# A routed two-block kernel: expert results loaded group by group as their units land, with four result buffers

## The chip, the cores and the metric

The kernel runs on one core of a Trainium2 chip. Its engines work side by side: PE (TensorE, matrix products), ACT (ScalarE), DVE (VectorE), POOL (GpSimd) and SP (SyncE, which here only issues transfers); each executes its own program in order and waits on semaphores. The metric is the device time of one execution in microseconds (us), lower is better. 1% is 4.5 us.

## The reference, cut to what matters

The input is 16 sequences of 256 tokens (4096 tokens) of 128 numbers. Two blocks follow one another, each of the form `x = x + s * silu(experts)`, with `s` from an attention-like part and the experts chosen per token, two of eight. The change touches the second block's expert part and its end:

```python
def _L1_ffn_ref(x, Wg, W1, b1, W2, b2):          # F = 512, E = 8, K = 2
    P = softmax(einsum('bsd,de->bse', x, Wg))
    _, topk_idx = top_k(P, 2)
    P_norm = P restricted to the two chosen, divided by their sum
    h = gelu(einsum('bsd,edf->ebsf', x, W1) + b1)
    y_e = einsum('ebsf,efd->ebsd', h, W2) + b2
    return einsum('ebsd,bse->bsd', y_e, P_norm)
...
g = silu(_L1_ffn_ref(xn, ...)); x = x + s * g
```

With the given inputs the eight experts are chosen 1096, 830, 727, 1419, 1359, 728, 1148 and 885 times. A unit is 256 rows of one expert, so they take 5, 4, 3, 6, 6, 3, 5 and 4 units, 36 in all.

## The kernel before

**Routing.** The tokens are handled in 8 groups of 512. For each group the layer norm of the second block gives rows that POOL scatters, through an indirect DMA, into the DRAM tensor `routed`, where each expert has a region. Each token goes to two experts; the one with the lower number is choice 0, the other choice 1. All of this, with the first block and the attention part of the second, lies in the *first pass*, a list called `ORDER` that every engine walks; the first unit of each expert (units 0 to 7) is worked in its last third.

**The loop over units.** The other units follow expert by expert in loops whose bounds are read from a table that DVE writes (`make_table`): expert 6 has units 6 and 29 to 32, expert 7 has units 7 and 33 to 35. For a unit `u`: SP loads its rows into one of the 4 slots of `ring` (L490), once `ring_free` says that the unit four before is done with its slot. DVE copies them to `xu` (`take`, L1610), two units ahead. PE transposes them (L1019) and makes the hidden layer (L1029, `hid`), ACT applies Gelu (L1239), PE makes the second product into `psC` (L1041, `out`; in the first pass `psB`, L1052). The order on PE is hid(u), transpose for u+1, out(u-1). DVE then runs `results_of`: it adds the bias from `psC` to `yb` (L1622), which frees `psC` by `yb_ready`; waits until the buffer of two units before has landed (`y_landed`); reads the rows' places (`y_to`, L1629) and weights (`y_wt`, L1632), which frees the ring's slot; and multiplies by the weights into `yw` (two operations, L1638). POOL then scatters both halves of 128 rows to the DRAM tensor `results` (L703), by choice and token, and counts in `y_landed` that the unit before has landed (L709).

**The ending.** SP issues two dummy loads of the ring (for takes that nobody uses), waits for them, and then, once the units of experts 0 to 6 have landed, loads choice 0 of all eight groups (`res_lower`, L572; 256 KB each) over first-layer weights that are no longer needed. When the last unit has landed (`all_landed`, L728) it loads choice 1 of all eight groups (`res_higher`). PE adds the two in PSUM through a product with the unit matrix (L1090 for choice 0, L1093 for choice 1, each a 128x512 product in two passes), ACT applies Silu (L1267), DVE multiplies with `s1` (L1665) and adds to `x_all` (L1667), and SP writes the group out (L581).

## Time and profile before

| | us |
|---|---|
| median of 3 runs (446.58, 450.25, 451.49) | 450.25 |
| the profiled execution, device time | 446.94 |
| its span in the trace | 445.2 |
| PE busy | 409.0 (92%) |
| DVE busy | 284.5 (64%) |
| ACT busy | 213.8 (48%) |
| POOL busy | 155.7 (35%) |

The span is the time from the first to the last instruction in the trace; 1.7 us of the device time lie outside it. The page cuts the span into 40 slices of 11.1 us: PE is busy for nine tenths or more in nearly all of them, at a granted clock of 1.0 of full speed, up to the last three. Busy time of PE is modelled, so what waits for what is read from the timeline and from the chain of waits.

### The profile page before, as it was taken

How to read it: one execution, taken by the hardware profiler on the slowest of the kernel's cores; microseconds unless marked ns; L12 is line 12 of the kernel's file. 1: busy time of each engine (PE TensorE's matmuls, PEld its weight loads, DVE VectorE, ACT ScalarE, POOL GpSimd, SP SyncE). 2: the span in 40 equal slices, each digit the busy share in tenths (PEclk: the TensorE clock that was granted, in tenths of full speed). 3: DMA queues.
4: the chain of work that ended last, by engine and by line, in shares of the span. 5: the costliest groups of instructions: out<-in, count | busy, mean ns of one | idle time of the engine just before them, and what ended most of it. 6: DMA issues, size and time to landing. Idle time of an engine off the chain costs nothing. (4 is left out here: it accounts for less than half of the span.)

```text
span 445.2 us, 9851 instructions
## 1 busy us (share of the span) xinstructions
PE 409.0 (92%) x2944; PEld 344.6 (77%) x2944; DVE 284.5 (64%) x1137; ACT 213.8 (48%) x525; POOL 155.7 (35%) x215
## 2 busy tenths in 40 slices
PE   7699989999999999999988999888999999999882
PEld 7579777878869779787767779777899999998630
DVE  4889889888887878878867657412233343433327
ACT  3364555565554545543424353333555555555412
POOL 6340015013233340443433011534454555455510
PEclk9999999999999999999999999999999999999998
DMA  7449411154064330131222223321222222222576
GB/s 181 123 114 166 57 40 42 50 170 135 13 192 122 81 79 25 47 83 53 75 54 61 66 51 80 101 80 54 68 71 67 78 71 71 61 77 68 169 275 193
DMA packets 64210, 40.80 MB, mean 92 GB/s; under 512 B 18340, under 2 KB 57128, under 8 KB 64168
## 3 DMA queue, kind: packets, MB, share of 16 engines
q1 hardware_dynamic: 59472, 31.27, 28.2%
q0 software_dynamic: 4352, 8.99, 6.1%
q8 instruction: 21, 0.34, 0.3%
q14 instruction: 21, 0.17, 0.1%
q10 hardware_dynamic: 344, 0.03, 0.1%
HBM read 21.78 MB, written 18.48 MB: 90 GB/s over the span
## 5 line engine op out<-in xcount | busy, mean ns | idle before, releaser
L694 POOL DMA_INDIRECT routed<-send,slot x64 | 64.5, 1008 | 129.1 <-DMA routed<-send,slot 57.5
L703 POOL DMA_INDIRECT results<-nat,y_to x72 | 69.8, 969 | 89.0 <-DVE nat L1638 65.4
L1029 PE MATMUL psA<-xuT,w_all 128*128 128x256 f32 x288 | 68.9, 381 | 3.5 <-ACT h1T L1239 3.2
L1239 ACT ACTIVATE h1T<-psA,b1T 128x256 f32<-128x256 f32 x144 | 63.1, 473 | 12.0 <-PE psB L1052 7.5
L1029 PEld LDWEIGHTS psA<-xuT,w_all 128*128 128x128 f32 x288 | 50.6, 190 | 11.5 <-issue 2.9
L1041 PE MATMUL psC<-w_all,h1T 128*128 128x128 f32 x464 | 56.7, 275 | 1.0 <-DVE nat L1622 1.0
L1610 DVE TENSOR_SCALAR xu<-ring 128x256 f32 (+1 forms) x38 | 11.2, 295 | 71.2 <-DMA ring<-routed 67.0
L1041 PEld LDWEIGHTS psC<-w_all,h1T 128*128 128x128 f32 x464 | 54.1, 192 | 1.3 <-ACT h1T L1239 1.1
L1230 ACT ACTIVATE xuT<-psB 128x256 f32<-128x256 f32 x37 | 14.2, 383 | 61.6 <-PE psB L1019 45.8
L843 PE MATMUL psB<-xnT,w_l 128*128 128x512 f32 x64 | 34.3, 618 | 0.0
L1170 ACT ACTIVATE hg0T<-psB,b1T 128x512 f32<-128x512 f32 x32 | 22.0, 688 | 22.9 <-PE psB L845 22.8
L855 PE MATMUL psB<-w_l,hg0T 128*128 128x128 f32 x256 | 32.7, 281 | 0.2 <-ACT hg0T L1170 0.2
L855 PEld LDWEIGHTS psB<-w_l,hg0T 128*128 128x128 f32 x256 | 31.2, 192 | 1.1 <-ACT hg0T L1170 0.6
L845 PEld LDWEIGHTS psB<-selT,expert_of 128*128 128x128 bf16 x128 | 9.8, 98 | 18.3 <-issue 18.3
L1638 DVE TENSOR_SCALAR nat<-nat,y_wt 128x128 f32 (+1 forms) x72 | 17.5, 283 | 7.7 <-issue 5.6
L1177 ACT ACTIVATE gg<-psB,tok_w 128x128 f32<-128x128 f32 x32 | 9.1, 368 | 25.3 <-PE psB L856 25.3
L746 PE MATMUL psC<-ident 128*128 128x128 f32 x136 | 19.7, 295 | 1.7 <-POOL ident L598 1.7
L746 PEld LDWEIGHTS psC<-ident 128*128 128x128 f32 x136 | 18.2, 209 | 2.3 <-POOL ident L598 1.7
L683 POOL COPY send<-send 128x512 f32<-128x512 f32 x8 | 5.4, 675 | 40.5 <-ACT send L1105 28.6
L1325 DVE BATCH_NORM_STATS2 stats<-x_all 128x6 f32<-128x128 f32 x64 | 13.9, 279 | 5.8 <-DMA x_all<-in_L_attn_x_dram 5.6
L1105 ACT ACTIVATE send<-x_all,shift,rstd 128x128 f32<-128x128 f32 x32 | 13.2, 483 | 8.6 <-DVE shift L1342 6.5
L1622 DVE TENSOR_TENSOR nat<-psC,b_all 128x256 f32<-128x256 f32 x29 | 12.2, 420 | 4.1 <-PE psC L1041 3.7
(289 smaller groups left out, 851.8 us busy)
## 6 DMA issues: line engine op xcount, KB each, us to landing
ring<-routed SPq DMA_DIRECT2D x38, 130.0 KB
inv<-inv_room SPq DMA_DIRECT2D x8, 512.0 KB
w_all<-results SPq DMA_DIRECT2D x15, 256.0 KB, 4.1
routed<-ring SPq DMA_DIRECT2D x24, 130.0 KB, 6.7
n_room<-nT SPq DMA_DIRECT2D x8, 256.0 KB
w_all<-in_L_ffn_W_dram SPq DMA_DIRECT2D x1, 2048.0 KB
out_dram<-x_all SPq DMA_DIRECT2D x8, 256.0 KB, 2.3
results<-nat,y_to POOLq DMA_INDIRECT x72
```

The costliest lines, as they stand in the source:

```text
L694: pool.indirect_dma_start(routed[:, :], bass.IndirectOffsetOnAxis(ap=slot[par][:, c, t:t + 1], axis=0), send[par][:, c, t, :], None).then_ ...
L703: pool.indirect_dma_start(results[:, :], bass.IndirectOffsetOnAxis(ap=y_to[:, par, a:a + 1], axis=0), yw[:, par, a, :], None).then_inc(S[f ...
L746: mm(to, ident[:, :], ident[:, :], start=True, stop=True)
L843: mm(psB[:, j % 2, :], w, xT0[:, :], start=True, stop=False)
L855: mm(o, hg0T[:, j, col(t)], w2_l0[:, j, :], start=(j == 0), stop=False)
L1029: last = mm(psA[:, j // 2, (j % 2) * UNIT:(j % 2 + 1) * UNIT], w1_all[:, e, j * P:(j + 1) * P], xuT[:, :], start=True, stop=True)
L1041: last = mm(psC[:, a, 0:D], h1T[:, k, a * P:(a + 1) * P], w2_all[:, f * JF + k, :], start=(k == 0), stop=(k == JF - 1))
L1170: f(hg0T[:, j, :], psB[:, j % 2, :], ACT.Gelu, bias=b1T[:, HT + j:HT + j + 1]).then_inc(S["hg0_ready"], 1)
L1230: f(xuT[:, :], psB[:, 0, 0:UNIT], ACT.Copy).then_inc(S["xuT_ready"], 1)
L1239: f(h1T[:, j, :], psA[:, j // 2, (j % 2) * UNIT:(j % 2 + 1) * UNIT], ACT.Gelu, bias=b1T[:, n:n + 1]).then_inc(S["gelu_ready"], 1)
L1325: last = v.bn_stats(stats[:, first + t, :], x_all[:, x_first + t:x_first + t + 1, :])
L1638: last = v.tensor_scalar(yw[:, mine, a, :], yb[:, a:a + 1, :], y_wt[:, a:a + 1], None, ALU.mult)
```

## The change

1. **Result buffers**: `yw` has four buffers, not two. DVE waits for the buffer of four units before. `yb` becomes a tile of its own.
2. **`results_of` in another order**: places and weights are read first (the ring's slot is freed before the unit's second product is done), then bias times weight goes to `yb`, and once the product is there one operation per half gives `psC * weight + yb`. `psC` is now freed by the last of these (`yw_ready`), no longer by the bias operation. `yw_ready` counts halves; POOL waits for each half.
3. **The last unit** makes its first half completely, then its second (`half_ps`), and the halves are weighted and sent apart.
4. **Loads of results by group**: DVE notes after each group how many rows experts 6 and 7 hold (`held`) and works out, behind the table, how many units must have landed for each group (`reach`). SP reads these numbers and waits for each. The dummy ring loads are gone; their count is added to the semaphore. By the counts of this input, choice 0 of groups 0 to 7 needs 29, 30, 31, 31, 31, 32, 33, 33 landed units (the last two by the rule that expert 6 must be finished), choice 1 needs 33, 34, 34, 34, 35, 35, 36, 36.
5. **The ending**: group 0 is summed by DVE in SBUF; groups 1 to 7 by PE, the choice 0 part of group 1 ahead of the last unit's second product. ACT writes Silu over the first-layer weights; DVE finishes groups 2 and 3, and 4 and 5, in one operation each (`ENDS`). After group 0 DVE fills the places of up to three dummy units, so that POOL's loop can go in rounds of four; this waits for the count 35. With 36 units POOL sends none of them.

In the tail of PE's program, with names as in the code (`w_all` is the tile of weights over which results are loaded), this stands in before:

```order
L394 REGISTER_ALU
L1041 MATMUL psC<-w_all,h1T 128x128 [waits gelu_ready]
L1041 MATMUL psC<-w_all,h1T 128x128
L394 REGISTER_ALU
L1041 MATMUL psC<-w_all,h1T 128x128 [waits gelu_ready]
L1041 MATMUL psC<-w_all,h1T 128x128
L1090 MATMUL psD<-w_all,ident 128x512 [waits s1_ready,lower_in0]
L1090 MATMUL psD<-w_all,ident 128x512 [waits lower_in1]
```

and this now:

```order
L1136 MATMUL psD<-w_all,ident 128x512 [waits s1_ready,lower_in1]
L409 ISA
L409 ISA [waits yw_ready]
L1079 MATMUL psC<-w_all,h1T 128x128 [waits gelu_ready]
L409 REGISTER_ALU
L1079 MATMUL psC<-w_all,h1T 128x128 [waits gelu_ready]
L409 REGISTER_ALU
L1079 MATMUL psC<-w_all,h1T 128x128 [waits gelu_ready]
L409 REGISTER_ALU
L1079 MATMUL psC<-w_all,h1T 128x128 [waits gelu_ready]
L1079 MATMUL psC<-w_all,h1T 128x128 x4
L1136 MATMUL psD<-w_all,ident 128x512 [waits lower_in2]
```

The choice 0 product of group 1 has moved ahead of the last unit's second product, which now waits for `yw_ready` in place of `yb_ready`; the others still follow it, group 0 has none.

DVE's operations for a unit in the loop of expert 7 stood like this in before (`ISA` and `REGISTER_ALU` rows set registers):

```order
L1610 TENSOR_SCALAR xu<-ring 128x256
L394 ISA
L1622 TENSOR_TENSOR nat<-psC,b_all 128x256 [waits yw_ready,h1_free]
L1629 ISA [waits y_landed]
L1629 ISA
L1629 TENSOR_SCALAR y_to<-ring 128x2
L1632 ISA
L1632 TENSOR_SCALAR y_wt<-ring 128x2
L394 REGISTER_ALU
L394 REGISTER_ALU [waits ring_free]
L1638 ISA [waits yb_ready]
L1638 TENSOR_SCALAR nat<-nat,y_wt 128x128
```

and stand like this now:

```order
L1689 ISA [waits y_landed,yw_ready]
L1689 ISA
L1689 TENSOR_SCALAR y_to<-ring 128x2
L1692 ISA
L1692 TENSOR_SCALAR y_wt<-ring 128x2
L409 REGISTER_ALU
L1697 TENSOR_SCALAR yb<-b_all,y_wt 128x128 [waits ring_free]
L1697 TENSOR_SCALAR yb<-b_all,y_wt 128x128
L409 ISA [waits yb_ready]
L1705 ISA [waits h1_free]
L1705 SCALAR_TENSOR_TENSOR nat<-psC,y_wt,yb 128x128
```

Places, weights and the bias product now stand ahead of the wait for the second product (`h1_free`), and that wait stands directly ahead of the operations that read `psC` (a second pair of rows like the last two follows).

The diff, cut to its core:

```diff
@@ -559,23 +575,39 @@
                     load_unit(u, nc.s_assert_within((u - bounds[e] + FIRST_UNITS) * UNIT + e * REGION,
                                                     e * REGION, e * REGION + tokens))
-            load_unit(bounds[E], 0)
-            load_unit(bounds[E] + 1, 0)
-            wait_on(sp, "unit_in", (bounds[E] + 2) * 16)
+            wait_on(sp, "unit_in", bounds[E] * 16)
             sp.sem_inc(apart, 1)
-            def load_results(c, to, signal):
-                for g in range(groups):
-                    at = c * tokens + g * GW
-                    sp.dma_start(to[g], results[at:at + GW, :].rearrange("(p t) d -> p t d", t=TILES)
-                                 ).then_inc(signal[g], 16)
+            sp.sem_inc(S["unit_in"], 2 * 16)
+            def load_results(c, g, to, signal):
+                at = c * tokens + g * GW
+                sp.dma_start(to[g], results[at:at + GW, :].rearrange("(p t) d -> p t d", t=TILES)
+                             ).then_inc(signal[g], 16)
+            def units_for(g, c):
+                return sp.value_load(reach[0:1, 2 * g + c:2 * g + c + 1], min_val=FIRST_ALL, max_val=MAX_UNITS)
+            sp.wait_ge(reach_ready, 1)
+            for g in range(groups - 2):
+                wait_on(sp, "y_landed", units_for(g, 0))
+                sp.sem_inc(apart, 1)
+                load_results(0, g, res_lower, lower_in)
+            wait_on(sp, "y_landed", units_for(0, 1))
+            sp.sem_inc(apart, 1)
+            load_results(1, 0, res_higher, res_in)
             wait_on(sp, "y_landed", bounds[E - 1])
-            load_results(0, res_lower, lower_in)
-            sp.wait_ge(all_landed, 1)
-            load_results(1, res_higher, res_in)
+            sp.sem_inc(apart, 1)
+            for g in range(groups - 2, groups):
+                load_results(0, g, res_lower, lower_in)
+            for g in range(1, groups - 1):
+                wait_on(sp, "y_landed", units_for(g, 1))
+                sp.sem_inc(apart, 1)
+                load_results(1, g, res_higher, res_in)
+            wait_on(sp, "y_landed", bounds[E])
+            sp.sem_inc(apart, 1)
+            load_results(1, groups - 1, res_higher, res_in)
             for g in range(groups):
                 sp.wait_ge(S["x2_ready"], g + 1)
                 sp.dma_start(out_rows[:, g * TILES:(g + 1) * TILES, :],
...
-            def send_results(u, par):
-                wait_on(pool, "yw_ready", u + 1)
-                pool.sem_inc(apart, 1)
+            def send_results(u, buf):
                 for a in range(HALVES):
+                    wait_on(pool, "yw_ready", u * HALVES + a + 1)
+                    pool.sem_inc(apart, 1)
                     pool.indirect_dma_start(
-                        results[:, :], bass.IndirectOffsetOnAxis(ap=y_to[:, par, a:a + 1], axis=0),
-                        yw[:, par, a, :], None).then_inc(S[f"y_sent{par}"], 16)
+                        results[:, :], bass.IndirectOffsetOnAxis(ap=y_to[:, buf, a:a + 1], axis=0),
+                        yw[:, buf, a, :], None).then_inc(S[f"y_sent{buf}"], 16)
                 if not (isinstance(u, int) and u == 0):
-                    pool.wait_ge(S[f"y_sent{1 - par}"], (u + par) * (8 * HALVES))
+                    pool.wait_ge(S[f"y_sent{(buf - 1) % YBUFS}"], (u - buf + (YBUFS if buf else 0)) * (16 * HALVES // YBUFS))
                     pool.sem_inc(S["y_landed"], 1)
             def unit_work(what, k=0):
...
-            with pool.Fori(FIRST_ALL, pairs_end, 2) as u:
-                send_results(u, 0)
-                send_results(u + 1, 1)
-            pool.wait_ge(S["y_sent1"], pairs_end * (8 * HALVES))
-            pool.sem_inc(all_landed, 1)
+            rounds_end = pool.value_load(table[0:1, 2 * E + 1:2 * E + 2], min_val=FIRST_ALL,
+                                         max_val=MAX_UNITS + YBUFS - 1)
+            assert FIRST_ALL % YBUFS == 0
+            with pool.Fori(FIRST_ALL, rounds_end, YBUFS) as u:
+                for buf in range(YBUFS):
+                    send_results(u + buf if buf else u, buf)
+            pool.wait_ge(S[f"y_sent{YBUFS - 1}"], rounds_end * (16 * HALVES // YBUFS))
+            pool.sem_inc(S["y_landed"], 1)
...
@@ -1034,7 +1069,20 @@
             def out(u, f, e):
-                wait_on(pe, "yb_ready", u)
+                wait_on(pe, "yw_ready", u * HALVES)
+                if e is None:
+                    for a in range(HALVES):
+                        for k in range(JF):
+                            if a == 0:
+                                wait_on(pe, "gelu_ready", u * JF + k + 1)
+                            last = mm(psC[:, a, 0:D], h1T[:, k, a * P:(a + 1) * P],
+                                      w2_all[:, f * JF + k, :], start=(k == 0), stop=(k == JF - 1))
+                            if a == HALVES - 1:
+                                last.then_inc(S["h1_free"], 1)
+                        if a == 0:
+                            last.then_inc(half_ps, 1)
+                    return
                 for k in range(JF):
                     wait_on(pe, "gelu_ready", u * JF + k + 1)
                     for a in range(HALVES):
...
@@ -1077,18 +1125,21 @@
                     bounds.extend(unit_bounds(pe, len(bounds), upto))
             first_pass(pe, work, unit_work)
-            other_units(pe, bounds, hid, out)
-            for g in range(groups):
+            def lower(g):
                 pe.wait_ge(lower_in[g], 16)
-                if g == 0:
+                if g == 1:
                     wait_on(pe, "s1_ready", groups)
-                elif g == 4:
+                elif g == 5:
                     pe.wait_ge(S["xuT_ready"], bounds[E] + 1)
-                elif g == 6:
-                    wait_on(pe, "yb_ready", bounds[E])
+                elif g == 7:
+                    wait_on(pe, "yw_ready", bounds[E] * HALVES)
                 mm(sum_ps_of(g), ident[:, :], res_lower[g], start=True, stop=False)
-            for g in range(groups):
+            other_units(pe, bounds, hid, out, lambda: lower(1))
+            for g in range(2, groups):
+                lower(g)
+            for g in range(1, groups):
                 pe.wait_ge(res_in[g], 16)
                 mm(sum_ps_of(g), ident[:, :], res_higher[g], start=False, stop=True).then_inc(S["sum_ps"], 1)
...
+            act.wait_ge(sum_sb, 1)
+            f(mix1(0, 1), mix1(0, 1), ACT.Silu).then_inc(S["silu1_ready"], 1)
+            for g in range(1, groups):
+                act.wait_ge(S["sum_ps"], g)
+                f(w1_all[:, g, :], sum_ps_of(g), ACT.Silu).then_inc(S["silu1_ready"], 1)
         @block.vector
...
@@ -1542,6 +1592,8 @@
                     link(v.tensor_tensor(pick[:, :, c], choice[:, :, c], twice(place[:, :, :]), ALU.mult))
                     link(v.tensor_reduce(slot_f[:, :, :], pick[:, :, c], AX.X, ALU.add))
                     v.tensor_copy(slot[par][:, :, :], slot_f[:, :, :]).then_inc(S["slots_ready"], 1)
+                    if g < groups - 1:
+                        link(v.tensor_copy(held[:, g, :], filled[0:1, E - 2:E]))
                     if g == groups - 2:
...
+                def per_group(m):
+                    return m.unsqueeze(1).broadcast_to([1, groups - 1, 2])
+                link(v.tensor_tensor(reach_f[:, :, :], held[:, :, :], per_group(region0[0:1, E - 2:E]), ALU.subtract))
+                link(v.tensor_scalar(held_i[:, :, :], reach_f[:, :, :], float(UNIT - 1), None, ALU.add))
+                link(v.tensor_scalar(held_i[:, :, :], held_i[:, :, :], UNIT.bit_length() - 1, None,
+                                     ALU.logical_shift_right))
+                link(v.tensor_scalar(reach_f[:, :, :], held_i[:, :, :], float(FIRST_UNITS), -float(FIRST_UNITS),
+                                     ALU.max, ALU.add))
+                v.tensor_tensor(reach[:, :].rearrange("a (p e) -> a p e", e=2), reach_f[:, :, :],
+                                per_group(bound_f[:, E - 2:E]), ALU.add).then_inc(reach_ready, 1)
             def take(u):
...
@@ -1615,17 +1679,13 @@
                 dve.wait_ge(S["xuT_ps"], u + 2)
                 take(u + 2)
-            def results_of(u, f, ps):
-                wait_on(dve, "h1_free", (u + 1) * JF)
-                wait_on(dve, "yw_ready", u)
-                v.tensor_tensor(yb[:, :, :], ps,
-                                b2_all[:, f:f + 1, :].broadcast_to([P, HALVES, D]),
-                                ALU.add).then_inc(S["yb_ready"], 1)
-                wait_on(dve, "y_landed", u - 1)
+            def results_of(u, f, ps, by_halves=False):
+                wait_on(dve, "yw_ready", u * HALVES)
+                wait_on(dve, "y_landed", u - YBUFS + 1)
                 at = ring[:, bass.ds(u % RING, 1), :, :]
-                mine = bass.ds(u % 2, 1)
+                mine = bass.ds(u % YBUFS, 1)
                 v.tensor_scalar(y_to[:, mine, :].rearrange("p r a -> p (r a)").unsqueeze(2),
                                 at[:, :, :, COL_ID:COL_ID + 1].bitcast(I32)
                                 .rearrange("p r a d -> p (r a) d"), 0.0, None, ALU.add)
@@ -1633,11 +1693,17 @@
                                 .rearrange("p r a d -> p (r a) d"), 1.0, None,
                                 ALU.mult).then_inc(S["ring_free"], 1)
                 wait_on(dve, "ring_free", u + 1)
+                for a in range(HALVES):
+                    last = v.tensor_scalar(yb[:, a, :], b2_all[:, f, :], y_wt[:, a:a + 1], None, ALU.mult)
+                last.then_inc(S["yb_ready"], 1)
                 wait_on(dve, "yb_ready", u + 1)
                 for a in range(HALVES):
-                    last = v.tensor_scalar(yw[:, mine, a, :], yb[:, a:a + 1, :], y_wt[:, a:a + 1],
-                                           None, ALU.mult)
-                last.then_inc(S["yw_ready"], 1)
+                    if a == 0 and by_halves:
+                        dve.wait_ge(half_ps, 1)
+                    else:
+                        wait_on(dve, "h1_free", (u + 1) * JF)
+                    v.scalar_tensor_tensor(yw[:, mine, a, :], ps[:, a:a + 1, :], y_wt[:, a:a + 1], yb[:, a:a + 1, :],
+                                           ALU.mult, ALU.add).then_inc(S["yw_ready"], 1)
             def unit_work(what, k=0):
                 if what == "first":
...
+            def spare_places():
+                wait_on(dve, "yw_ready", bounds[E] * HALVES)
+                for n in range(YBUFS - 1):
+                    wait_on(dve, "y_landed", bounds[E] + n - YBUFS + 1)
+                    mine = bass.ds((bounds[E] + n) % YBUFS, 1)
+                    v.tensor_scalar(y_to[:, mine, :].rearrange("p r a -> p (r a)").unsqueeze(2),
+                                    spare[:, mine, :].rearrange("p r a -> p (r a)").unsqueeze(2), 0.0, None,
+                                    ALU.add).then_inc(S["yw_ready"], HALVES)
+            dve.wait_ge(lower_in[0], 16)
+            dve.wait_ge(res_in[0], 16)
+            v.tensor_tensor(mix1(0, 1), mix1(0, 1), res_higher[0], ALU.add).then_inc(sum_sb, 1)
+            def finish(first, end):
+                ts = slice(first * TILES, end * TILES)
+                m = mix1(first, end)
+                dve.wait_ge(S["silu1_ready"], end)
+                v.tensor_tensor(m, s1[:, ts, :], m, ALU.mult).then_inc(S["mix_ready"], end - first)
+                dve.wait_ge(S["mix_ready"], end)
+                v.tensor_tensor(x_all[:, ts, :], x_all[:, ts, :], m, ALU.add).then_inc(S["x2_ready"], end - first)
             dve.wait_ge(S["s1_ready"], groups)
-            for g in range(groups):
-                finish(g)
+            for first, end in ENDS:
+                finish(first, end)
+                if first == 0:
+                    spare_places()
 # ---- launch: one core; inputs and outputs as the reference has them ----
```

## Rows read from the trace of the kernel before

**Rows 1.** windows at the end: us, busy us (x instructions), clock, DMA share
```profile
400.00:420.00 20.00, 19.04 (x136) 17.18 (x135) 7.27 (x32) 12.23 (x27) 10.23 (x11) 1.00 0.31 93
420.00:430.00 10.00, 7.37 (x17) 2.58 (x16) 1.14 (x5) 0.00 (x0) 3.32 (x4) 1.00 0.71 240
```

**Rows 2.** chain that ended last, in time order: start us, us, what
```profile
424.79 2.24 DMA results<-nat,y_to
...
427.09 2.77 DMA w_all<-results
...
429.91 1.14 PE psD L1093 x2
...
431.07 0.61 ACT hg0T L1267
...
431.77 0.70 DVE hg0T L1665
...
441.79 0.69 DVE x_all L1667
```

**Rows 3.** timeline of SP and PE at the end: start us, us, what
```profile
417.06 3.45 SPq L572 DMA_DIRECT2D w_all<-results  x7
...
417.84 2.05 PE L1041 MATMUL psC<-w_all,h1T 128*128 128x128 f32 x16 [0.96 <-DVE nat L1622]
...
426.20 1.02 PE L1090 MATMUL psC<-w_all,ident 128*128 128x512 f32 x2
...
427.06 1.02 PE L1090 MATMUL psC<-nT,ident 128*128 128x512 f32 x2
```

**Rows 4.** timeline, DVE and POOL around the last two units
```profile
417.31 0.97 POOL L703 DMA_INDIRECT results<-nat,y_to  x1 [0.30 <-issue]
...
418.19 0.48 DVE L1638 TENSOR_SCALAR nat<-nat,y_wt 128x128 f32 x2 [0.24 <-DVE y_wt L1632]
...
419.46 0.97 POOL L703 DMA_INDIRECT results<-nat,y_to  x1 [1.19 <-issue]
...
419.92 0.42 DVE L1622 TENSOR_TENSOR nat<-psC,b_all 128x256 f32<-128x256 f32 x1 [1.25 <-PE psC L1041]
...
420.74 0.96 POOL L703 DMA_INDIRECT results<-nat,y_to  x1 [0.30 <-issue]
421.70 0.17 DVE L1629 TENSOR_SCALAR y_to<-ring  x1 [1.35 <-issue]
```

**Rows 5.** one line of the ending: duration ns min/median/max
```profile
L1665 DVE TENSOR_TENSOR hg0T<-s,hg0T x8: 682/684/691, 431.8 to 441.1; 128x512 f32<-128x512 f32 x8
```

**Rows 6.** timeline, the loop over units: PE, DVE, SP
```profile
321.25 1.95 PE L1041 MATMUL psC<-w_all,h1T 128*128 128x128 f32 x16
...
322.81 0.29 DVE L1610 TENSOR_SCALAR xu<-ring 128x256 f32 x1 [1.91 <-DMA ring<-routed]
...
324.99 1.95 PE L1041 MATMUL psC<-w_all,h1T 128*128 128x128 f32 x16
...
407.43 0.38 SPq L490 DMA_DIRECT2D ring<-routed  x1
...
410.34 0.29 DVE L1610 TENSOR_SCALAR xu<-ring 128x256 f32 x1 [2.39 <-DMA ring<-routed]
...
414.93 1.95 PE L1041 MATMUL psC<-w_all,h1T 128*128 128x128 f32 x16
```

**Rows 7.** timeline, from the first pass into the loop
```profile
306.97 0.30 DVE L1610 TENSOR_SCALAR xu<-ring 128x256 f32<-128x256 f32 x1 [4.87 <-DMA ring<-routed]
...
308.47 1.95 PE L1052 MATMUL psB<-w_all,h1T 128*128 128x128 f32 x16
```

**Rows 8.** page, groups of instructions and DMA issues
```profile
L1638 DVE TENSOR_SCALAR nat<-nat,y_wt 128x128 f32 (+1 forms) x72 | 17.5, 283 | 7.7 <-issue 5.6
...
w_all<-results SPq DMA_DIRECT2D x15, 256.0 KB, 4.1
```

**Rows 9.** timeline of SP, the eight fills
```profile
283.81 8.66 SPq L544 DMA_DIRECT2D routed<-fill  x8
```

68 lines of the change are left out of this document (32 added, 36 removed).

## The prediction

> **What bounds the kernel now.** I read the windows first. Up to 420 us PE is busy nearly without a gap at a granted clock of 1.00, which is the level of 2.4 GHz; from 420 to 430 us it still works for 7.4 us, DVE for 1.1 and ACT for none [rows 1]. So there are two parts: a long one set by PE, and an ending of some 25 us set by something else. The chain of waits says by what [rows 2]: the last scatter of results (issued at 424.79, landed 2.24 us later), the load of choice 1 of the first group (2.77), PE's sum (1.14), Silu (0.61), and then DVE alone: from 431.77 to 442.48 (441.79 + 0.69) it alternates between the two operations of each group. That is 10.71 us for 8 groups, 1.33 a group plus 0.07 for the last dependency. The write of the last group takes the rest of the span, 445.2 - 442.48 = 2.72 us. All eight loads of choice 1 wait for the last unit, although most groups' rows have landed long before; that is where time can be had. The sum below is made on the span (445.2 us); the profiled execution took 446.94.
>
> **The long part.** Four edits act before the last unit.
>
> *The order inside a unit.* In the loop PE starts a second product every 3.75 us (321.25 to 414.93 in 25 periods [rows 6]). DVE's take starts 1.56 us after the start of the product at 321.25; the one at 410.34 is among the late ones, its load issued at 407.43 had taken 2.91 us [rows 6]. Freeing the slot earlier makes this chain shorter: the 0.42 us bias operation no longer stands in it. Only few tenths are there to win, because an undisturbed period is 324.99 - 321.25 = 3.74, and 25 of them are 93.5 us against 93.7 measured. I take -0.2 (bounds -0.4 and 0).
>
> *`psC` comes free later.* Between take and free there now stand places and weights, two bias products and two operations on PSUM. Nearest rows: 128x256 from PSUM 0.42 [rows 4], 128x512 from two tiles 0.68 [rows 5], so 0.27 for 256 columns and about 0.285 for 128; two of them 0.55. A small operation is 0.17 [rows 4], a weighting 0.283 [rows 8]. Take 0.29, two small ones 0.3, two waits on its own results about 0.5, two bias products 0.5, the last pair 0.55: about 2.15 us. Where the take is not late, all but the last pair lies under PE's product (1.95 us), and the pair lies under the hidden product, the other 1.8 us of the period; cost zero. Where the take comes x us after the product's start, PE waits once x + 2.15 exceeds 3.74. That is so at one place that the trace shows: the take at 306.97 had waited 4.87 us for its ring slot's rows, and PE began the next product at 308.47 [rows 7]. Now the bank is free at 306.97 + 2.15 = 309.1: +0.6 us. After it the take falls in step, since from take to take by way of a load it is now about 0.5 to the weights, 0.25 to SP (both estimated from the small operations) and 2.91, under 3.74.
>
> *DVE's additions in the first pass*: seven notes of `held`, five operations for `reach`, and per unit about 0.2 us more (0.57 + 0.57 for the two pairs instead of 0.42 + 0.57, and waits). With 0.25 us each that is 1.75 + 1.25 + 1.4 = 4.4 us on DVE. PE keeps busy beside it, so most is hidden; bounds 0 and 4.4, I take +0.2, nearer to nothing since the `reach` operations stand behind the signal that others wait for.
>
> *Ahead of the last product* the choice 0 sum of group 1 (two passes, 1.02 us; groups on PE stand 0.86 apart) goes where PE waited 0.96 us for `psC`, from 416.9 to 417.84 [rows 3]. The last product starts at 417.9, not 417.84: +0.1.
>
> Sum of the long part: -0.2 + 0.6 + 0.2 + 0.1 = +0.7 us. The last product ends at 420.6 instead of 419.9.
>
> **The ending.** *Scatter.* Unit 34's halves are ready at about 418.1 (416.9 + 0.6 for the shift, 0.55 for the pair), POOL starts them 0.8 later as now (418.19 + 0.48 to 419.46 [rows 4]): 418.9 and, a send taking 1.27 with its gap (419.46 to 420.74), 420.1. The last unit's first half is ready 1 us before the end, at 419.9; POOL is free at 421.3, sends at 421.3 and 422.5. It lands 2.24 later [rows 2], or later when loads share the DMA engines: DVE got the buffer of unit 33, whose second half was sent at 417.31, only at 421.70 [rows 4], 4.39 us later, while eight loads were under way from 417.06 [rows 3]. (That reading is an upper bound: POOL may have counted late.) So the last unit has landed at 424.8 to 426.9; before it was 427.03. The wait of DVE on the buffer (1.35 us [rows 4]) is gone with four buffers.
>
> *Loads.* The SP queue is done with the ring when the last real load has landed, at 410.3 at the latest [rows 6], so choice 0 goes out from then to about 417, and choice 1 of group 0 at about 417. Each dynamic step (a read of `reach`, a wait, an issue) I price by the eight fills, 8.66/8 = 1.08 us [rows 9]; bare issues are 3.45/7 = 0.49 [rows 3]. Groups 1, 2, 3 need 34 units, counted at 420.0 to 420.9: issued by 420.9, 422.0, 423.1. Groups 4 and 5 need 35: 424.2, 425.3. Groups 6 and 7: 426.4 to 427.0, and 0.5 later. Landing is 2.77 for the first [rows 2], 4.1 in the median [rows 8]: groups 1 to 7 are there at 425.0, 426.1, 427.2, 428.3, 429.4, 431.0, 431.6 at the latest.
>
> *PE* has six choice 0 sums to do after 420.6: 6 x 0.86 = 5.2, to 425.8. Then choice 1 of group 1: result at 425.8 + 1.14 = 426.9, the others 0.86 apart, kept back by at most 1 us by the loads.
>
> *DVE* does group 0 (sum 0.69, Silu 0.6, two products) from 421.0 to 423.6 and the spare places (three of 0.17 with register work) to 424.3; the count 35 for which they wait is there by 424.3. It is then idle until Silu of group 1, 426.9 + 0.65 = 427.5. From there: group 1 1.33 (428.8); groups 2 and 3, whose Silu is ready at 429.2: an operation of 1024 columns is 0.68 + 2 x 0.27 = 1.22, two with their dependency 2.4 (431.6); groups 4 and 5 2.4 (434.0); group 6 1.33, group 7 1.40 (436.7). The write 2.72: **439.4**.
>
> So the span falls by 445.2 - 439.4 = 5.8 us: 4.3 because DVE's row starts at 427.5 and not 431.8, 1.5 because it has seven groups and two of its steps are doubled. The profiled execution would take 446.94 - 5.8 = 441.1. The median of the runs shown is 450.25, 3.3 above that execution, with one run (446.58) at its level; scaled by 439.4/445.2 it is 444.4. I say 443.5, between the two and nearer to the scaled median.
>
> **One rule against it.** Scatters and loads delay each other: 2.24 us alone, up to 4.39 beside eight loads [rows 2, 4]. The Trainium skill ("DMA: Bandwidth & Descriptors", section "Issuing engines are not separate DMA queues") says that transfers of all queues run on the same 16 DMA engines and interleave; the trace agrees with 4.39 beside 2.24. The old ending kept the last scatter free of loads, the new one puts it among those of groups 1 to 5. By 2.24 the last group is loaded at 430.1, by 4.39 at 431.6; DVE comes to it at 435.3, which needs the load by 433.5, so both give 439.4.
>
> **Rivals.** (a) *The hidden work of DVE isn't hidden*: in the first pass all 4.4 us lie on the path, or PE waits for `psC` more often. Against it: PE's few gaps there. It gives 439.4 + 4.2 on the span: 445 to 449 by the runs, within 1%. (b) *The last landing decides.* From a landing of group 7 after 433.5, two microseconds past my latest, each further us costs one. The rule above is its mechanism; a scatter of 6.5 us would eat 1 to 2 us: 445. (c) *Slower*: `psC` late in every unit. If a take stays more than 1.59 us behind the product's start, PE waits for the excess each time; at 2.0 behind that is 0.42 x 28 = 12 us, 450.25 + 6 = 456. It needs ring loads that land over 2.98 us after issue in the mean, where the late one took 2.91 [rows 6]; and each such wait gives the loads time to catch up. (d) *More than forecast*: the ring's chain is what makes two of three runs 450 and more; shortened, it takes away 3 us besides: 440. For it the late take at 410.34 [rows 6], against it that no row shows such a loss. (e) *The counts don't come early*, so that the loads go out late as before: all choice 1 loads would again follow the last unit's landing. Against it: two groups of eight need the last unit, the rest up to two units less. It would leave some 2.5 us of the faster scatter and the 1.5 of DVE: 446.
>
> **How the numbers follow.** My forecast 50% (own range 441 to 446.5), (a) 15%, (b) and (e) together 10%, (c) 8%, (d) 17%. The range 438 to 449 leaves out (c) and the far ends of (a) and (d). About 1% (4.5 us) is what a measurement can tell from no change. Faster by over 1%: (d) and most of my forecast, 0.60. Within: the rest of it, (a), (b), (e): 0.32. Slower: 0.08.
>
> **What would show it.** In the profile after: DVE's last row of operations starts near 427.5 + 0 to 1 and lasts 9.2 us without a wait for a DMA (else (b)); PE's first choice 1 sum stands right behind the last choice 0 sum; the start of PE's last product lies near 418.5 (at 422: (a); at 430: (c)); loads of choice 1 go out in three bunches. I am wrong if PE shows waits for DVE's `psC` in the loop, or if its idle time before the choice 1 sums exceeds 1 us each.

## The result: slower by 1.3%, with the ending faster as forecast and the loop slower

The changed kernel takes 453.75 us in the median of 14 runs (451.81 to 457.15), the kernel before 447.88 (445.42 to 451.49, 14 runs). The ratio is 1.0129, 95% interval 1.0098 to 1.016. The forecast was 443.5 (438 to 449) with a chance of 0.08 for slower by over 1%: it was wrong, in sign too. The profiled execution of the changed kernel has a span of 451.6 us, against 445.2.

Where the 6.4 us of span come from, place by place (starts of the same product in both traces):

| place | before | after | cost |
|---|---|---|---|
| first unit's product of the loop starts | 312.7 | 314.95 | +2.3 |
| from there to the loop's 28th product | 102.1 | 112.4 | +10.2 |
| from the 28th to the end of the span | 30.4 | 24.3 | -6.1 |

So the change gained 6.1 us where it was meant to gain, and I had forecast 5.8 for the whole. The loop lost 10.2 us, where I had forecast -0.2. First the ending, in the timeline of the changed kernel; columns as in the same view of before (start us, us, engine and line, what, [idle before <- releaser]); DVE's last line of operations answers [rows 2], the loads [rows 3]:

```profile
430.45 2.05 PE L1079 MATMUL psC<-w_all,h1T 128*128 128x128 f32 x16 [0.22 <-ACT h1T L1290]
...
432.66 7.08 SPq L585 DMA_DIRECT2D w_all<-results  x7
...
434.75 1.13 POOL L737 DMA_INDIRECT results<-nat,y_to  x1 [0.30 <-issue]
...
437.48 1.88 PE L1144 MATMUL psD<-w_all,ident 128*128 128x512 f32 x4
...
439.17 0.69 DVE L1744 TENSOR_TENSOR w_all<-s,w_all 128x512 f32<-128x512 f32 x1 [2.97 <-ACT w_all L1318]
...
440.88 1.13 PE L1144 MATMUL psA<-w_all,ident 128*128 128x512 f32 x2 [0.66 <-DMA w_all<-results]
...
440.96 1.23 DVE L1744 TENSOR_TENSOR w_all<-s,w_all 128x1024 f32<-128x1024 f32 x1 [0.37 <-ACT w_all L1318]
...
448.12 0.69 DVE L1746 TENSOR_TENSOR x_all<-x_all,w_all 128x512 f32<-128x512 f32 x1
```

From the start of the last product to the end of the span it is 451.6 - 430.45 = 21.15 us; before it was 445.2 - 417.84 = 27.36 [rows 3]. PE's first choice 1 sum (437.48) stands behind the last choice 0 sum (436.62, two passes) with no wait, and the only wait of the row on a load is 0.66. DVE's row lasts 448.81 - 439.17 = 9.64 (forecast 9.2), the write 2.79 (forecast 2.72).

Now the loop. One unit of it, in the changed kernel and in the kernel before (the product on `psC` is the second product of the unit before, the one on `psA` the hidden product of the next):

```profile
381.74 1.87 PEld L1089 LDWEIGHTS psC<-w_all,h1T 128*128 128x128 f32 x16
...
382.35 0.96 POOL L737 DMA_INDIRECT results<-nat,y_to  x1 [0.30 <-issue]
...
383.65 2.32 PE L1064 MATMUL psA<-xuT,w_all 128*128 128x256 f32 x8
383.95 0.84 ACT L1290 ACTIVATE h1T<-psA,b1T 128x256 f32<-128x256 f32 x2 [0.35 <-PE psC L1089]
...
384.84 0.73 PEld L1064 LDWEIGHTS psA<-xuT,w_all 128*128 128x128 f32 x4 [0.46 <-ACT h1T L1290]
```

```profile
321.25 1.95 PE L1041 MATMUL psC<-w_all,h1T 128*128 128x128 f32 x16
...
321.90 1.81 ACT L1239 ACTIVATE h1T<-psA,b1T 128x256 f32<-128x256 f32 x4
322.97 0.98 POOL L703 DMA_INDIRECT results<-nat,y_to  x1 [0.30 <-issue]
```

In the kernel before, ACT's four Gelus follow one another with no gap (1.81 for four): each overwrites a quarter of `h1T`, and PE's releases of the quarters (`h1_free`, one at the end of each quarter of the product) come in time. In the changed kernel ACT waits for the third release: 0.35 us in the row, and PE then waits 0.46 for ACT's result. I count time in a unit from the first weight load of the product (here 381.74; 0.10 before the row of the matmuls). The releases are due at +0.74, +1.18, +1.63 and +2.07, and where nothing is late ACT starts a Gelu some 0.02 us behind each. The matmul of the third ends at +1.63, but its signal arrives at +2.14, and ACT's third Gelu starts at +2.21. Half a microsecond is lost in most units: the median period is 4.15 in place of 3.73. The rows that group this, ACT's Gelus between 310 and 415 us (form, count | busy, mean ns | idle before <- releaser), of before and of after:

```profile
L1239 ACT ACTIVATE h1T<-psA,b1T 128x256 f32<-128x256 f32 x112 | 50.3, 473 | 3.6 <-PE psC L1041 1.3 <-PE psB L1052 0.8
```

```profile
L1290 ACT ACTIVATE h1T<-psA,b1T 128x256 f32<-128x256 f32 x100 | 44.0, 472 | 14.9 <-PE psC L1089 11.4 <-issue 1.4
```

ACT's waits for `psC` have grown from 1.3 to 11.4 us, the 10.2 of the loop. I call such a release late. Nothing in my working had a price for it, and PE's rows show no wait for DVE there, which is what I had feared in rival (c).

The 2.3 us ahead of the loop are not the change's, or hardly. Of this execution 1.6 us went into one stretch in which the clock granted to PE was lower (behind it the same operations of DVE stand 1.6 us later than in the two further profiles named below, ahead of it they do not):

```profile
20.00:25.00 5.00, 4.86 (x23) 4.00 (x24) 4.50 (x20) 3.98 (x8) 4.73 (x20) 0.67 0.00 0
```

(windows: us, busy us of PE, PEld, DVE, ACT, POOL, clock, DMA share, GB/s; in the kernel before the clock reads 1.00 there.) In two more profiles of the unaltered changed kernel it reads 1.00 there, and the first product of the loop starts at 312.5 and 312.3, where the kernel before has 312.7.

### The profile page after: what moved, and what is told of

Its sections match the earlier page's. It is cut to its first block, busy times and chain, and to the rows that moved or that the text cites. A ratio compares the mean times of both kernels' runs of the same rounds, so it can differ in the third digit from the quotient of the medians.

```text
span 451.6 us, 10024 instructions
## 1 busy us (share of the span) xinstructions
PE 415.5 (92%) x2940; PEld 345.2 (76%) x2940; DVE 302.2 (67%) x1185; ACT 212.9 (47%) x525; POOL 154.3 (34%) x216
## 4 chain that ended last, share of the span: by engine, by line
PE 61%; DVE 16%; issue 8%; ACT 6%; SPq 4%; DMA 3%; ACTq 1%; DVEq 0%
PE psC L1089 12%; PE psA L1064 10%; PE psB L890 7%; PE psB L878 6%; ACT h1T L1290 2%; DVE stats L1375 2%; DMA ring<-routed 2%; PE psD L1007 2%; PE psB L1054 1%; PE psB L880 1%; PE psA L846 1%; DVE nt_a L1389 1%; PE psC L781 1%; PE psA L860 1%; DVE nt_a L1390 1%
## 5 line engine op out<-in xcount | busy, mean ns | idle before, releaser
L728 POOL DMA_INDIRECT routed<-send,slot x64 | 63.5, 993 | 131.4 <-DMA routed<-send,slot 56.3
L1064 PE MATMUL psA<-xuT,w_all 128*128 128x256 f32 x288 | 75.8, 393 | 6.8 <-ACT h1T L1290 4.7
L1674 DVE TENSOR_SCALAR xu<-ring 128x256 f32 (+1 forms) x38 | 12.5, 329 | 64.0 <-PE psB L1054 47.1
L1089 PE MATMUL psC<-w_all,h1T 128*128 128x128 f32 x448 | 54.6, 275 | 0.0
L1089 PEld LDWEIGHTS psC<-w_all,h1T 128*128 128x128 f32 x448 | 52.2, 192 | 0.0
L1705 DVE SCALAR_TENSOR_TENSOR nat<-psC,y_wt,yb 128x128 f32 x58 | 17.9, 347 | 9.8 <-PE psC L1089 8.8
L1697 DVE TENSOR_SCALAR yb<-b_all,y_wt 128x128 f32<-128x128 f32 x72 | 17.5, 291 | 1.3
```

The costliest lines, as they stand in the source:

```text
L728: pool.indirect_dma_start(routed[:, :], bass.IndirectOffsetOnAxis(ap=slot[par][:, c, t:t + 1], axis=0), send[par][:, c, t, :], None).then_ ...
L1064: last = mm(psA[:, j // 2, (j % 2) * UNIT:(j % 2 + 1) * UNIT], w1_all[:, e, j * P:(j + 1) * P], xuT[:, :], start=True, stop=True)
L1089: last = mm(psC[:, a, 0:D], h1T[:, k, a * P:(a + 1) * P], w2_all[:, f * JF + k, :], start=(k == 0), stop=(k == JF - 1))
L1697: last = v.tensor_scalar(yb[:, a, :], b2_all[:, f, :], y_wt[:, a:a + 1], None, ALU.mult)
L1705: v.scalar_tensor_tensor(yw[:, mine, a, :], ps[:, a:a + 1, :], y_wt[:, a:a + 1], yb[:, a:a + 1, :], ALU.mult, ALU.add).then_inc(S["yw_read ...
```

## The experiments

Eighteen runs were made in five groups, each group on one chip beside the kernel before; five of them repeat a kernel (the changed kernel twice, e1, e2 and e5 once each). The kernel before took 448.2, 448.7, 449.5, 449.6 and 447.3 us on them, which is no difference worth a word. The variants were another matter. Results in one table; "second send" is the place in a unit where POOL starts its second scatter of results, counted as above (its median, or the range that holds 8 units in 10).

| label | chip | ratio to before [95%] | median period | second send |
|---|---|---|---|---|
| e1_old_order | 10 | 0.986 [0.981, 0.991] | 3.73 | +1.5 to +2.3 |
| e2_bias_behind | 10 | 0.989 [0.984, 0.994] | 3.73 | +1.40 |
| e3_slot_late | 10 | 1.021 [1.016, 1.027] | 4.37 | +1.68 |
| e5_order_alone | 10 | 1.0005 [0.997, 1.004] | 3.73 | +1.15 |
| e0_after | 13 | 1.011 [1.008, 1.013] | 4.15 | +0.61 |
| e6_sends_whole | 13 | 1.021 [1.017, 1.025] | 4.36 | +0.9 to +1.2 |
| e8_sends_later | 13 | 1.041 [1.039, 1.044] | 4.64 | +1.47 |
| e9_slot_after_bias | 13 | 1.012 [1.007, 1.017] | 4.17 | +0.6 to +1.6 |
| e1_again | 6 | 1.007 [1.003, 1.011] | 4.03 | +1.57 |
| e2_again | 6 | 1.043 [1.037, 1.048] | 4.64 | +1.44 |
| e5_again | 6 | 1.039 [1.034, 1.044] | 4.43 | +0.88 |
| e7_old_by_halves | 6 | 1.024 [1.019, 1.028] | 4.20 | +0.61 |
| e10_sends_past | 5 | 1.007 [1.003, 1.010] | 4.43 | +2.03 to +2.2 |
| e11_old_sends_past | 5 | 0.997 [0.993, 0.9998] | 3.73 | +2.1 to +3.2 |
| e12_sends_spaced | 5 | 1.046 [1.039, 1.052] | 4.31 | spaced |
| e13_after_third | 5 | 1.013 [1.005, 1.021] | 4.20 | +0.61 |
| e14_sends_pinned | 7 | 0.988 [0.984, 0.991] | 3.73 | +2.94 |
| e15_old_pinned | 7 | 0.987 [0.983, 0.990] | 3.73 | +2.95 |

### First group (chip 10): which part of the change costs the period?

**e1_old_order** puts the order of DVE's steps in a unit back; four buffers, sends by halves, the loads by group and the new ending stay. The diff is shortened.

```diff
-                v.tensor_scalar(yb[:, a, :], b2_all[:, f, :], y_wt[:, a:a + 1], None, ALU.mult)   # bias first
+                v.tensor_tensor(yb, ps, b2_all[f], ALU.add).then_inc(S["yb_ready"], 1)            # frees psC
 ...
-                v.scalar_tensor_tensor(yw[a], ps[a], y_wt[a], yb[a], ALU.mult, ALU.add)
+                v.tensor_scalar(yw[a], yb[a], y_wt[a], None, ALU.mult)
```

> The changed kernel with one part undone: the weighting of a unit is again in the order of before (bias added from psC as soon as the product is there, which frees psC; then places, weights, two weightings). Four buffers, sending by halves, loads by group and the new ending stay. The traces show the loop's period at 3.74 us before and 4.13 after, some 10.6 us over 27 units, while the ending from the start of the last product is 6.2 us shorter (27.4 to 21.2). If the order inside a unit is the cause, the period goes back to 3.74 to 3.78 and the time falls below before by 5 to 7 us: ratio 0.984 to 0.990. If instead the four buffers, POOL's two waits per unit or the loop in rounds of four slow the loop, the period stays at 4.1 and the ratio at 1.01 or above.

Measured: 441.2 us, period 3.73, span 438.5. It looked like a proof that DVE's order makes the release late. And it tests the ending of the forecast with the loop undisturbed: 438.5 against the 439.4 of my sum.

```profile
417.62 1.95 PE L1079 MATMUL psC<-w_all,h1T 128*128 128x128 f32 x16
...
426.25 0.69 DVE L1751 TENSOR_TENSOR w_all<-s,w_all 128x512 f32<-128x512 f32 x1 [1.71 <-ACT w_all L1318]
...
435.02 0.69 DVE L1753 TENSOR_TENSOR x_all<-x_all,w_all 128x512 f32<-128x512 f32 x1
```

DVE's row starts 8.6 us behind the start of the last product (forecast 427.5 - 418.5 = 9.0) and lasts 9.46 (forecast 9.2).

**e2_bias_behind** keeps the new order, but DVE waits for PE's product before it makes the two bias products.

```diff
+                wait_on(dve, "h1_free", (u + 1) * JF)
                 for a in range(HALVES):
                     last = v.tensor_scalar(yb[:, a, :], b2_all[:, f, :], y_wt[:, a:a + 1], None, ALU.mult)
```

> The changed kernel, but DVE waits for the unit's second product before it multiplies the bias by the weights; places and weights are still read early, so the ring slot is freed and SP's load is issued inside PE's product as in the changed kernel. In its trace PE's signal for the third quarter of the product (h1_free) comes 0.5 to 0.58 us late in each unit, while both the two bias products of DVE and SP's issue of the ring load (0.38 us) run. Theory 1 (DVE's bias products delay the signal): the period goes back to 3.74 to 3.80, the time to 5 to 7 us under before, ratio 0.984 to 0.990. Theory 2 (SP's issue delays it): the period stays at 4.1, ratio 1.01 or a little above, since psC comes free 0.5 us later besides.

Measured: 442.2 us, period 3.73. Here SP's issue stands where it stood in the changed kernel, so it could not be the cause; the bias products could.

**e3_slot_late** frees the ring slot only behind the last operation of a unit.

```diff
-                                ALU.mult).then_inc(S["ring_free"], 1)
+                                ALU.mult).then_inc(S["wt_read"], 1)
 ...
+                dve.sem_inc(S["ring_free"], 1)
```

> The changed kernel, but the ring slot is declared free only after the unit's two last operations, so that SP issues the next load outside PE's second product; the bias products stay inside it. Theory 1 (bias products): the signal stays late by 0.5 us and the period at 4.1 us, ratio about 1.01. Theory 2 (SP's issue): the signal comes in time and the period goes back to 3.74 to 3.80, ratio 0.985 to 0.99.

Measured: 457.5 us, period 4.37, and for a reason that neither theory named: no release is late, the ring is. PE waits for `psC` in most units (22 waits, 9.6 us in all, between 310 and 415 us). One of them:

```profile
361.49 2.05 PE L1089 MATMUL psC<-w_all,h1T 128*128 128x128 f32 x16 [0.24 <-DVE nat L1705]
...
363.60 0.29 DVE L1674 TENSOR_SCALAR xu<-ring 128x256 f32 x1 [2.25 <-DMA ring<-routed]
...
365.15 0.61 DVE L1705 SCALAR_TENSOR_TENSOR nat<-psC,y_wt,yb 128x128 f32 x2 [0.25 <-DVE yb L1697]
...
365.89 0.37 PE L1089 MATMUL psC<-w_all,h1T 128*128 128x128 f32 x1 [0.41 <-DVE nat L1705]
```

This is my rival (c) as it was written, brought about on purpose: the take stands 2.11 us behind the product's start, `psC` is free 2.16 us behind the take (365.76; I had worked out 2.15), and PE waits for the excess. In the changed kernel the slot is freed early and the take comes 0.6 behind the start, so it does not happen there.

**e5_order_alone** is the kernel before with the new order of DVE's steps and nothing else.

> The kernel before with one part of the change alone: the new order of places, weights, bias products and the two operations on psC; two buffers, whole units sent, the old loads and the old ending. If the order is the cause (theories 1 and 2 alike) the period is 4.1 us and the time 9 to 12 us over before, ratio 1.02 to 1.027, with the ending as before. If it needs the four buffers or the sends by halves too, the period stays at 3.74 and the ratio near 1.00.

Measured: ratio 1.0005, period 3.73 in all units but two, with the bias products inside PE's product. So the order alone cost nothing on this chip, order and four buffers together (the changed kernel, measured elsewhere) cost 0.42 a unit, and each alone was free. That did not fit any theory I had.

### Second group (chip 13): the sends

What else differs between those kernels is the place of POOL's sends in the unit. It hangs on when a result is ready, on how many buffers there are and on whether the halves are waited for one by one. The group moves the sends, and runs the changed kernel again.

> The changed kernel once more, unaltered, on the chip that also runs the others of this group. The four variants run so far had no late release from PE, the profiles of the kernel before and of the changed one both had some, and those two came from other executions, perhaps another chip. Theory A (the change itself makes PE's third release of each second product late): period 4.15 in the loop, 1.3% above the kernel before (about 454). Theory B (the late releases belong to the chip or the execution, not to the kernel): no late release here, period 3.73, and with the ending's gain about 442.

> The changed kernel, but POOL waits for both halves of a unit before it sends either, as before the change. Its sends start about 0.3 us later in each unit: the second one ends near +1.9 us after the product's start instead of +1.58, where PE's third release is due at +1.63. Theory A1 (the release is late when POOL's send ends just before it): the release is on time or the lateness moves to the fourth release, period 3.73 to 3.9, 442 to 447. Theory A2 (four buffers or DVE's order as such): period stays 4.15, 454.

> The changed kernel, with one read of a word of the table on POOL (about 0.7 us, its value is not used) ahead of each loop unit's first send. Nothing is left out. The second send then runs from about +1.35 to +2.3 us after the product's start, past PE's third release at +1.63, as in the variants without late releases. Theory A1: no late release, period 3.73, about 442 (the ending may lose 1 us: the last unit's sends also start later). Theory A2: period stays 4.15, 454. Theory B: as the unaltered kernel does on this chip.

> The changed kernel, but the ring slot is freed behind the two bias products instead of ahead of them, so SP's issue comes at about +2.05 us after the product's start instead of +1.79, behind PE's third release; POOL's sends and the bias products keep their places. Theory A3 (SP's issue in the 0.2 us behind the release makes it late): release on time, period 3.73 to 3.8, 442 to 445. Theory A4 (the bias products there make it late, SP has no part): period stays 4.15, 454.

The edits: `e0_after` none. The other three:

```diff
 # e6_sends_whole, POOL
+                wait_on(pool, "yw_ready", (u + 1) * HALVES)
                 for a in range(HALVES):
-                    wait_on(pool, "yw_ready", u * HALVES + a + 1)
 # e8_sends_later, POOL, ahead of a unit's first send
+                        pool.value_load(table[0:1, 2 * E + 1:2 * E + 2], ...)
 # e9_slot_after_bias, DVE, behind the two bias products
+                dve.sem_inc(S["ring_free"], 1)
```

Measured: the changed kernel again 4.15, so it was not one odd execution; that the chip has a part in it, the other half of B, is not settled by this group. Both kernels with later sends are slower still, 4.36 and 4.64, so A1 as I had put it falls, and with the slot freed later it stays at 4.17, so A3 falls. But the trace of e8 said more than the time: now it is the fourth release that is late, by 0.95 us, and the third is not.

### Third group (chip 6): the same kernels on another chip

All four of the first group had no late release, all four of the second had some. So three of the first group ran again.

> The first variant (changed kernel with the old order of DVE's steps in a unit) once more. All four variants of the first group ran on one chip and none had a late release from PE in its trace, all four kernels of the second group ran on another chip and all had some. Theory K (it is the kernel's order that decides): again no late release that reaches PE, period 3.73, ratio to the kernel before 0.986. Theory C (it is the chip that decides): on a chip other than the first one, releases of PE are up to 1 us late here too, period 3.9 to 4.2, and the ratio rises to about 1.00 to 1.01.

> The second variant (changed kernel, bias products only behind the wait for PE's product) once more. Theory K: period 3.73, ratio 0.989. Theory C: on a chip other than the first one, late releases and a ratio of 1.00 or more.

> The kernel before with the new order of DVE's steps alone, once more. Theory K: ratio 1.00, period 3.73, no late release. Theory C: on a chip other than the first one, late releases that now reach PE, because DVE's step comes later in the unit: period about 4.1, ratio up to 1.02.

> As the run before it (kernel before, new order of DVE's steps), and the unit's results signalled and sent by halves: POOL's first send starts about 0.3 us earlier in each unit, with two buffers. If sends by halves are what makes the order expensive, this one has late releases and a period of about 4.1 while the one before it does not; if not, both stand at the same period.

Theory C holds, by a wide margin: e2 goes from 0.989 to 1.043, e5 from 1.0005 to 1.039, e1 from 0.986 to 1.007, with the same program. One unit of e2 on chip 10, then on chip 6:

```profile
362.08 1.87 PEld L1089 LDWEIGHTS psC<-w_all,h1T 128*128 128x128 f32 x16
...
362.83 1.81 ACT L1290 ACTIVATE h1T<-psA,b1T 128x256 f32<-128x256 f32 x4
...
363.47 0.97 POOL L737 DMA_INDIRECT results<-nat,y_to  x1 [0.30 <-issue]
```

```profile
361.22 1.86 PEld L1089 LDWEIGHTS psC<-w_all,h1T 128*128 128x128 f32 x16
...
361.97 1.37 ACT L1290 ACTIVATE h1T<-psA,b1T 128x256 f32<-128x256 f32 x3
...
362.65 0.97 POOL L737 DMA_INDIRECT results<-nat,y_to  x1 [0.30 <-issue]
...
364.26 0.47 ACT L1290 ACTIVATE h1T<-psA,b1T 128x256 f32<-128x256 f32 x1 [0.92 <-PE psC L1089]
364.78 0.73 PEld L1064 LDWEIGHTS psA<-xuT,w_all 128*128 128x128 f32 x4 [1.04 <-ACT h1T L1290]
```

POOL's second send is at +1.4 in both. On chip 10 four Gelus run in a row; on chip 6 the fourth waits 0.92 us, and PE after it 1.04. And two kernels of one group differ by their sends only: e5_again has its second send at +0.88 and a period of 4.43, e7 (the same, by halves) at +0.61 and 4.20.

What the chips differ in can be read off the signals that the traces record. I took the events of the loop of all 20 traces and counted them from the start of the second of two sends that follow each other by 1.27 us (pairs 1.25 to 1.30 us apart, whose first send starts between 318 and 410 us); "landing" is a signal of one of a transfer's 16 DMA engines.

| | chips 13, 6, 5, and the first profiles of before and after (14 traces) | chips 10, 7 (6 traces) |
|---|---|---|
| landings of the first send, +0.5 to +1.05 | 3 to 6 recorded (medians) | 16 (9 in e14, where some come later) |
| landings of the second send, near +2.1 (POOL at rest) | 16 | 16 (9 in e2 and 4 in e5, where they come later) |
| signals of any engine or DMA recorded, +0.92 to +1.38 | none in 288 of 291 pairs | some in all 125 |
| PE's releases of all products due +0.6 to +1.3 | 291 of 317 recorded late, near +1.5 to +1.6; 18 without a record | all 144 on time |

On one kind of chip the landing of the first send falls into the running second send, a few of its signals are recorded, and then no signal of anything is recorded for some 0.6 us, until about +1.5 us behind the start of the second send. I call this the silence. A release of the second product that is due in it takes effect at its end: of 69 for which ACT was already waiting (due +0.92 to +1.38), 68 let ACT start late, by 0.34 us in the median.

But it is a silence of the record, and not of all signals. In the unit of the changed kernel shown above DVE's read of the weights ends at 382.93 + 0.35 = 383.28, which is +0.93 behind the second send (382.35). Its signal has no record, yet SP, which waits for it, goes on 0.03 us later and issues the ring's load, while PE's third release is still 0.3 us away:

```profile
383.52 0.38 SPq L506 DMA_DIRECT2D ring<-routed  x1
```

So it is wherever one can look, in the same 14 traces and the same window: 105 signals of DVE for which SP was waiting let it start 25 to 29 ns later, as on the other chips (28 ns); 36 of 41 Gelus for whose end PE was waiting let it start 50 to 52 ns later, as there; and 7 of 9 of PE's own signals of a transpose let ACT start 36 to 38 ns later. None of them has a record. Even outside the window records are missing: in the kernel before, the third release has none in 17 of the 26 units behind the first, and ACT starts its third Gelu on time, at +1.64 to +1.66, in all 26. A missing record thus does not show a late signal; what shows it is the start of the engine that waited. By that, the releases of the second product are late in the silence, and DVE's signals are not. Why these and not the others, the traces do not show.

The rule gives the periods of most kernels: in the changed kernel the second send starts at +0.61, the silence ends at +0.61 + 1.53 = +2.14, the third release was due at +1.63: 0.51 late, of which the period shows 0.42. In e2_again it is +1.44 + 1.58 = +3.02, the fourth was due at +2.07: 0.95 late, the period +0.91. It does not give that of e1_again (4.03): there the second send starts at +1.57 and the fourth release is due 0.50 behind it, ahead of the silence; in 10 of 12 such units it took effect near +0.8 behind the send, about when the first send lands, 0.3 us late. The Trainium skill ("DMA: Bandwidth & Descriptors", section "Why a DMA increments its semaphore by 16 and not by 1") says that all 16 engines post a signal for a transfer issued by GpSimd: the traces agree, with 16 recorded for most sends on one kind of chip, and on the other wherever POOL is at rest.

The kernel before is nearly indifferent to the chip. Its second send starts at +1.8 to +2.9 in most units, so that the silence lies behind the last release that ACT waits for (322.97 in the rows above is +1.82; the release was due at +2.07, 0.25 behind the send's start, where the silence has not begun). Its trace has the silence in all 23 pairs; of 27 releases due in it 17 are recorded late, 16 of them of the hidden product, which has slack, and none of the second product. Only the loop's first unit, ahead of these pairs, has late releases of that (a period of 4.73). In 13 units its fourth release is due up to 0.27 us behind the second send, and is on time in all: the lateness ahead of the silence that e1_again shows is not explained by the place of the send alone.

### Fourth group (chip 5): move the silence

> The changed kernel with two reads of a word of the table on POOL (0.72 us each, values not used) ahead of each loop unit's first send. The second send then starts near +2.15 us after the product's start and its silence lies at +2.95 to +3.7, behind the fourth release (+2.07) and on the hidden product, as in the kernel before. Theory S (the silence behind the second send, where a release falls in it, is the loss): period 3.73 to 3.8 on any chip, span 438.5 to 441 (the last unit's sends come up to 1.4 us later). Theory N (the silence is a sign of something else that slows this chip's variants): period stays at 4.1 or more where the changed kernel beside it has 4.15.

> The first variant (changed kernel, old order of DVE's steps) with one such read ahead of each loop unit's first send: the second send starts near +2.0 to +2.3. It had a period of 3.73 on the first chip and 4.03 on the third. Theory S: 3.73 to 3.8 here, ratio 0.985 to 0.99. Theory N: as on the third chip, ratio about 1.007.

> The changed kernel, but POOL starts a unit's second send only when its first has landed (some 2.1 us after its start instead of 1.27). If the silence hangs on a landing that falls into a running send, there is none behind the first landing now; the second landing (2.1 us behind the second send's start) falls into the next unit's first send, and the silence moves there, about 1.9 to 2.6 us behind the second send's start. If it hangs on the second send alone, it stays at 0.8 to 1.5 us behind that send's start. Time: not forecast to better than 440 to 465, it hangs on which releases fall into the silence.

> The changed kernel unaltered, once more, on the chip of this group. On a chip of the kind of the second and third: silence from 0.8 to 1.5 us behind each second send, period 4.15, ratio 1.01. On a chip of the kind of the first: no silence, period 3.73, span near 439 to 441, ratio 0.985 to 0.99, which is what the prediction gave.

The edits: two such reads on POOL ahead of each loop unit's first send in e10 (in the changed kernel), one in e11 (in e1), none in e13. In e12:

```diff
+                    if a == 1 and not isinstance(u, int):
+                        pool.wait_ge(S[f"y_sent{buf}"], (u - buf) * (16 * HALVES // YBUFS) + 16)
```

Measured. **e11**: 21 of 27 periods are 3.73 or 3.74 where e1 on chip 6 had a median of 4.03; the units that are not have a send outside its place (one period of 5.48, two of 4.36 and 4.52 at the start). Ratio 0.997 against 1.013 of the changed kernel beside it, 7 us less. That is the old order and the delay together; e1 without the delay did not run on this chip, and had 1.007 on chip 6, which leaves 1% for the delay if the two chips are alike. **e10** sits at the edge: its second send starts within 0.1 us of the fourth release, due at +2.07, and in 12 units that release arrived only near +2.85, about when the first send lands, while in the other units it was at most 0.15 late: periods of 4.43 to 4.57 beside others of 3.73 to 3.84. That is a second way to be late, the one of e1_again, which my window did not have, and the forecast of 3.73 to 3.8 failed by it. (The profiled execution of e10 is the slowest of its ten, 456.9 us against a median of 452.9.) **e12** answers in part what the silence hangs on: the second send started 3.0 to 3.1 us behind the first, so that now the second send of a unit and the first of the next stand 1.27 apart. The silence moved there, behind the next unit's first send, and the landings of the lone send gave none. So it does not hang on the second send of a unit, but on two sends 1.27 us apart, whichever they are. That what does it in them is the landing in the running send fits all pairs, but no run has it apart from this distance. The time was bad (1.046), since it fell on the third release again.

### Fifth group (chip 7): a send held in its place

```diff
+                if not isinstance(u, int):
+                    wait_on(pool, "h1_free", (u + 1) * JF + 1)
+                    pool.sem_inc(apart, 1)
                 for a in range(HALVES):
```

(and PE adds to `h1_free` behind the last product, so that the last units are not kept waiting; e14 is the changed kernel with this, e15 the same on e1.)

> The changed kernel, unaltered but for one wait: POOL starts a loop unit's first send only when PE has given its first release (+0.74 us) of the next unit's product, so that the sends of each unit start near +0.90 and +2.17 us and the silence lies at +2.97 to +3.7, behind the product's last release. Theory S: period 3.73 to 3.76 in nearly all units on either kind of chip, last product some 11 us earlier than in the changed kernel, span 439 to 442, ratio 0.98 to 0.99. Theory N, or if +2.17 is still too near to the release due at +2.07: period 4.1 or more in many units, ratio 1.00 or above.

> The first variant (changed kernel with DVE's old order) with the same wait. Theory S: as the run before it, span 438.5 to 441, ratio 0.98 to 0.985 on either kind of chip, since the order of DVE's steps costs nothing by itself. If DVE's order matters on its own on a slow chip, this one is faster than the run before it by more than 1%.

Measured: 442.2 and 441.7 us, 26 of 27 periods at 3.73 or 3.74 in both; the last product starts at 419.4 and 417.0 (forecast 418.5) and the spans are 441.2 and 439.8 (forecast 439.4). But chip 7 is of the kind without silence (signals recorded in every window), so this does not show that the wait cures the other kind. It shows two things: DVE's new order is free on such a chip (0.988 and 0.987), and the changed kernel's own loop and ending, with one wait of POOL added, run at 442 there. The sends also stood later than I had wanted, the second at +2.94 and not +2.17. I had forgotten what lies between POOL's wait and its send: in the unit of these rows the wait for PE's first release passed at 364.85 (+0.75), as meant, the next one at 365.02, and the send started 0.76 us behind that:

```profile
365.77 0.97 POOL L740 DMA_INDIRECT results<-nat,y_to  x1 [1.50 <-PE psC L1092]
367.04 0.97 POOL L740 DMA_INDIRECT results<-nat,y_to  x1 [0.30 <-issue]
```

**What stays open.** The unaltered changed kernel ran on chips 13 and 5, not on one without silence; e1, e2 and e14 at 0.986 to 0.989 make it likely, and no more, that it would be near 0.985 to 0.99 there. The pinned version was not run on a chip with silence; e11 is the best that was measured on one (0.997). Why releases of the second product are late in the silence while DVE's signals pass, and what makes some late ahead of it, is open. No chip was visited twice, so that "chip" could also be something else that held for a whole group. What in the chip makes the silence is not known.

## Why the prediction was wrong, point by point

- **The order inside a unit, -0.2, and "cost zero" for the bias products.** This is the step that failed: the loop cost +10.2 us. The durations were right and so was their place under PE's product; e5 on chip 10 and e14 show that on a chip without silence the order costs nothing by itself. What the step left out is what a result that is ready earlier does to the engine behind it. I followed DVE's operations and the slot, and not POOL's two sends, which the new order, the four buffers and the halves moved from +1.8 (322.97 against a product at 321.25 [rows 6]) to +0.61, where PE's third release falls into the silence. The kernels of chip 6 divide this up, and there the order is not free: alone it puts the second send at +0.88 (e5_again, period 4.43, ratio 1.039), with the halves at +0.61 (e7, 4.20); buffers and halves with the old order put it at +1.57 (e1_again, 4.03). I had named the halves only for the last unit. No row of before could have priced it: the lateness shows there only in the loop's first unit.
- **`psC` comes free later, +0.6.** Over-sized. From take to product it is 310.64 - 308.98 = 1.66 us, before 308.47 - 306.97 = 1.50 [rows 7]: +0.16. The 2.15 us that I had worked out from take to free are right in the loop (2.16 in e3), but in the units of the first pass the same steps take 1.61:

```profile
308.98 0.30 DVE L1674 TENSOR_SCALAR xu<-ring 128x256 f32<-128x256 f32 x1 [5.25 <-DMA ring<-routed]
...
309.98 0.61 DVE L1705 SCALAR_TENSOR_TENSOR nat<-psB,y_wt,yb 128x128 f32<-128x128 f32 x2
...
310.64 2.05 PE L1100 MATMUL psB<-w_all,h1T 128*128 128x128 f32 x16 [0.34 <-DVE nat L1705]
```

- **The first pass, +0.2.** Right as far as can be measured: the loop starts at 312.5 and 312.3 in the two further profiles, before at 312.7. Rival (a) falls.
- **The sum ahead of the last product, +0.1.** Right: 430.45 - 427.41 = 3.04, before 2.91 [rows 3, 6].
- **The ending.** Right: forecast 439.4 - 418.5 = 20.9 us from the last product's start to the end of the span, measured 21.15 and, in e1, 20.9. DVE's row was forecast to start 9.0 behind that start and did 8.7 and 8.6 behind it; its length was 0.3 to 0.4 under-sized. The loads of choice 1 go out from 432.66, 2.2 us behind that start (forecast 2.4), and PE's sums wait 0.66 us for them in all, so rivals (b) and (e) fall. The rule on scatters and loads changed nothing, as both of its sums had said: one wait of 0.66 us on a load.
- **Rival (c), slower.** The sign was right and, by luck, nearly the size (456 against 453.75); the mechanism was not: no wait of PE for DVE in the loop. I had given 0.08 to all that could go wrong in each of 28 units, and priced only the one way that the rows of before could show. Its point of decision was right, as e3 shows.
- **Rival (d).** Falls: no 3 us came from a shorter ring chain; where the loop is undisturbed (e1, e14) the time is 441 to 442, as in the sum.
- **The spread.** The first runs of before (446.58 to 451.49) were not two levels of the ring's making; 62 later runs, on five chips, spread from 445.9 to 453.0 with no second level in them.

## What to carry to other kernels

When a step makes a result ready earlier, follow it to the engine that fetches it, and list what will then stand beside what: a buffer more, or a wait less, is a change of phase for everything behind it. Where a loop has a chain of small handshakes (four releases and four Gelus in 1.8 us), half a microsecond on one signal is half a microsecond on the period, so one asks which of the signals has slack and puts the disturbing transfers beside those. A signal without a record in a trace is not a late signal: look at when the engine that waits for it starts. And a comparison in which each kernel ran on one chip only can give two opposite and seemingly clean answers: run the pair again elsewhere before a theory is built on it.

## What the runs showed of the hardware that I had not expected

- On three of five chips, a scatter's landing during POOL's next scatter is followed by some 0.6 us in which no signal of any engine or DMA is recorded (none in 288 of 291 pairs of sends, against signals in all 125 on the other two chips). Of PE's releases of the second product for which ACT waited, 68 of 69 took effect late (in e2 on chip 6 the fourth by 0.95 us); all 105 signals of DVE for which SP waited passed as fast as elsewhere.
- The same program is 5.4% slower on one chip than on another by the ratio to a kernel that is equally fast on both (e2: 0.989 and 1.043).
- A small operation of DVE that starts in the second half of POOL's send can last until just before the send ends: 0.35 us for the read of the weights in the changed kernel (`y_wt`, 382.93, to +0.93 of a send of 0.96) and 0.17 in e2, where no send runs. It is no sign of the loss: e1 on chip 10 has it too, with a period of 3.73.

```profile
382.93 0.35 DVE L1692 TENSOR_SCALAR y_wt<-ring 128x2 f32 x1
```

```profile
363.27 0.17 DVE L1692 TENSOR_SCALAR y_wt<-ring 128x2 f32 x1
```
